# Cross-attention scores of a perceiver layer: sixteen 32x32 fp32 tiles per batch in place of masked three-part matmuls

## The reference, cut to what matters

```
x = x + xattn(layernorm(x), ctx, ctx, mask, Wq, bq, Wk, bk, Wv, bv, Wo, bo)
q = (Q @ Wq.T + bq)  -> 16 heads of 32        # k, v from ctx in the same way
scores = q k^T / sqrt(32) + mask              # [batch, head, 32, 257]
out = softmax(scores) v ;  return out @ Wo.T + bo
```

## Time and profile before

| | us |
|---|---|
| median of 3 runs | 837.57 |
| the runs | 836.25, 837.57, 840.66 |
| the profiled execution, own time | 840.95 |
| its span | 838.9 |
| TensorE busy | 784.2 |
| VectorE busy | 468.3 |
| ScalarE busy | 336.2 |
| GpSimd busy | 301.8 |

### The profile page before, as it was taken

How to read it: one execution, slowest core, us unless ns; L and a number is a source line. 1 busy time by engine, 2 the same in 40 slices (tenths; PEclk the granted TensorE clock), 3 DMA queues, 4 the chain that set the end, 5 groups by cost and what they waited for, 6 DMA issues and landing times. The chain is left out here.

```text
span 838.9 us, 19731 instructions
## 1 busy us (share of the span) xinstructions
PE 784.2 (93%) x7618; PEld 632.4 (75%) x7618; DVE 468.3 (56%) x1000; ACT 336.2 (40%) x686; POOL 301.8 (36%) x375
## 2 busy tenths in 40 slices
PE   2999999999999999999999999769999988999994
PEld 1878888888888888888888887557888766677673
DVE  6725555636555554556465555555676676433556
ACT  2534435443443434344444435322554454622220
POOL 2038023303312330332133130455677671394002
PEclk9999999999999999999999999889999989999998
DMA  8111110110011011101101113130000003100011
GB/s 322 54 47 51 52 52 1 52 50 10 40 50 50 0 50 50 49 1 50 50 3 47 50 50 101 50 90 3 1 0 0 1 8 118 54 0 1 1 50 50
DMA packets 8455, 36.92 MB, mean 44 GB/s; under 512 B 2137, under 2 KB 2393, under 8 KB 5218
## 3 DMA queue, kind: packets, MB, share of 16 engines
q1 hardware_dynamic: 8418, 36.42, 12.1%
HBM read 34.32 MB, written 2.10 MB: 43 GB/s over the span
## 5 line engine op out<-in xcount | busy, mean ns | idle before, releaser
L94 PE MATMUL pj<-W_hi 128*128 128x512 f32 x512 | 206.6, 403 | 0.0
L96 PE MATMUL pj<-W_lo,W_hi 128*128 128x512 f32 x512 | 200.8, 392 | 0.0
L95 PE MATMUL pj<-W_hi,W_lo 128*128 128x512 f32 x512 | 199.7, 390 | 0.0
L640 DVE SCALAR_TENSOR_TENSOR kf_lo<-pj,bk,kf_hi 128x512 fp32r<-128x512 f32 x64 | 48.0, 750 | 120.5 <-ACT kf_hi L477 120.5
L96 PEld LDWEIGHTS pj<-W_lo,W_hi 128*128 128x128 f32 x512 | 96.1, 188 | 21.5
L94 PEld LDWEIGHTS pj<-W_hi 128*128 128x128 f32 x512 | 96.2, 188 | 18.4
L247 POOL CAST kf_hi<-kt_hi 128x8 fp32r (+1 forms) x32 | 6.3, 197 | 287.9 <-PE tp L96 278.4
L95 PEld LDWEIGHTS pj<-W_hi,W_lo 128*128 128x128 f32 x512 | 96.4, 188 | 17.5
L477 ACT ACTIVATE kf_hi<-pj,bk 128x512 fp32r<-128x512 f32 x64 | 44.2, 690 | 134.6 <-PE pj L96 134.6
L484 ACT ACTIVATE V<-pj 128x512 f32<-128x512 f32 x64 | 38.3, 599 | 107.4 <-PE pj L96 107.4
L492 ACT ACTIVATE p_flat<-m_flat,nmax 128x257 f32<-128x257 f32 x128 | 63.8, 501 | 11.6 <-DVE nmax L651 11.6
(11 more groups left out here) (283 smaller groups left out, 1609.7 us busy)
## 6 DMA issues: line engine op xcount, KB each, us to landing
raw<-ctx_dram SPq DMA_DIRECT2D x15, 1024.0 KB, 4.8
raw<-w_dram SPq DMA_DIRECT2D x5, 1024.0 KB, 4.8
raw<-w_dram SPq DMA_DIRECT2D x6, 768.0 KB, 4.3
out_dram<-raw SPq DMA_DIRECT2D x8, 256.0 KB, 2.1
x_nat<-x_dram SPq DMA_DIRECT2D x2, 512.0 KB, 4.7
raw<-wq_dram SPq DMA_DIRECT2D x1, 1024.0 KB, 7.1
x_nat<-x_dram SPq DMA_DIRECT2D x1, 1024.0 KB, 9.1
raw<-wk_dram SPq DMA_DIRECT2D x1, 1024.0 KB, 10.2
```

Of the source, the lines that this page charges most:

```text
L94: eng.matmul(out, a_hi, b_hi, start=first, stop=False)
L95: eng.matmul(out, a_lo, b_hi, start=False, stop=False)
L96: return eng.matmul(out, a_hi, b_lo, start=False, stop=last)
L640: eng.scalar_tensor_tensor(out=K_lo[:, g, :, 0:SM], in0=pj[g % 2][:, :].rearrange("p (j n) -> p j n", j=2), scalar=bk[:, g:g + 1], in1=K_h ...
```

## The change

Each batch's scores become sixteen fp32 matmuls, not split: for row group r (partitions 32r to 32r + 31, the head r of each group) and column group g, weights are 32 channels x 32 queries of `q_b`, the moving operand is 257 columns of K on the same 32 partitions. The result of (r, g) goes to bank `sc[r]`, rows 32g to 32g + 31. So a bank now holds the heads r, 4 + r, 8 + r, 12 + r in place of 4g to 4g + 3. The order is four rounds k, in each r = 0 to 3 with g = (r + k) mod 4; only the four matmuls of the last round raise `s_done`. They wait for all masks of the batch before at once.

What follows from the new order of heads: V's channels are placed by permuted views of Wv as it is split (four pieces in place of one on ScalarE and on VectorE), bv is loaded in four strips, and Wo's rows in four strips of 256 KB. K is kept as one fp32 tensor, evacuated by ScalarE alone; VectorE's `k_evac` and the split of the tail keys go. GpSimd's `q_blocks` becomes one copy per batch, beside one copy of the tail key. `wq_hi` and `wq_lo` get tensors of their own. The mask, softmax, transposes and weighted sum keep their code.

```diff
+        K = sb("K", [P, CT, 2, SK])
+        q_b = [sb(f"q_b{j}", [P, CT, S]) for j in range(2)]
+        def wv_by_tile(c):
+            return wv_raw[:, c, :].rearrange("p (g r d) -> p r g d", g=CT, r=4)
 # SyncE
-            eng.dma_start(bv[:, :], io["bv"]).then_inc(small_in, 16)
+            for g in range(CT):
+                strip, of_strip = bv[g * HD:(g + 1) * HD, :], io["bv"].rearrange("(r d) g -> g d r", d=HD)[g]
+                eng.dma_start(strip, of_strip, allow_slow_non_contiguous=True).then_inc(small_in, 16)
...
+            eng.wait_ge(ctx_lo, NPAIR - 1)
+            for g in range(CT):
+                strip = raw[g * HD:(g + 1) * HD, 0, :].rearrange("p (r n) -> p r n", r=CT)
+                of_strip = io["w5"][0].rearrange("(r d) (g n) -> g d r n", d=HD, g=CT)[g]
+                eng.dma_start(strip, of_strip).then_inc(wo_in, 16)
+            eng.wait_ge(ctx_lo, NPAIR)
+            eng.dma_start(raw[:, 1, :], io["w5"][1]).then_inc(w_in[1], 16)
 # GpSimd, pair(n)
-                need(eng, s_done, 8 * n)
...
+                if isinstance(n, int) and n == 0:
+                    eng.wait_ge(tailT_out, 2)
                 for j in range(2):
-                    for K, kt in ((K_hi, kt_hi), (K_lo, kt_lo)):
-                        eng.tensor_copy(K[:, :, j, SM:KW],
-                                        kt[:, :, bass.ds(2 * n + j, 1)].broadcast_to([P, CT, 2])).then_inc(k_tail, 1)
-                if not first:
-                    q_blocks(n, 0)
-                    q_blocks(n, 1)
+                    b = 2 * n + j
+                    need(eng, s_done, 4 * (b - 1))
+                    eng.tensor_copy(q_b[j][:, :, :], Q_T[:, :, bass.ds(b * S, S)]).then_inc(qb_made, 1)
+                    eng.tensor_copy(K[:, :, j, SM:SK], kt32[:, :, bass.ds(b, 1)]).then_inc(k_tail, 1)
 # TensorE, scores(n, j)
-                for g in range(CT):
-                    need(eng, masked_made, 8 * n + 4 * (j - 1) + g + 1)
-                    if g == 2 and j == 0:
-                        need(eng, pt_act, 2 * n)
-                        need(eng, pt_dve, 2 * n)
-                    three(eng, sc[g][:, 0:KW], Qd_hi[j][:, g, :], Qd_lo[j][:, g, :],
-                          K_hi[:, g, j, :], K_lo[:, g, j, :], True, True).then_inc(s_done, 1)
+                b = 2 * n + j
+                eng.wait_ge(k_out, 4 * n + 4)
+                eng.wait_ge(k_tail, b + 1)
+                eng.wait_ge(qb_made, b + 1)
+                need(eng, masked_made, 4 * b)
+                if j == 0:
+                    need(eng, pt_act, 2 * n)
+                    need(eng, pt_dve, 2 * n)
+                eng.sem_inc(s_ready, 1)
+                for k in range(4):
+                    for r in range(4):
+                        g, rows = (r + k) % CT, slice(r * HD, (r + 1) * HD)
+                        mm = eng.matmul(sc[r][g * S:(g + 1) * S, 0:SK], q_b[j][rows, g, :], K[rows, g, j, :], start=True, stop=True)
+                        if k == 3:
+                            mm.then_inc(s_done, 1)
 # ScalarE
-                eng.activation(K_hi[:, g, :, 0:SM], pj[g % 2][:, :].rearrange("p (j n) -> p j n", j=2),
-                               ACT.Identity, bias=bk[:, g:g + 1]).then_inc(k_hi, 1)
+                eng.activation(K[:, g, :, 0:SM], pj[g % 2][:, :].rearrange("p (j n) -> p j n", j=2),
+                               ACT.Identity, bias=bk[:, g:g + 1]).then_inc(k_out, 1)
...
-            split_hi(wv_hi[:, :, :], wv_raw).then_inc(w_hi, 1)
+            for c in range(CT):
+                split_hi(wv_hi[:, c, :].rearrange("p (r g d) -> p r g d", r=4, g=CT), wv_by_tile(c)).then_inc(wv_made, 1)
+            eng.wait_ge(wv_made, CT)
+            eng.sem_inc(w_hi, 1)
 # VectorE: split_lo of Wv in the same four pieces, and
-            def k_evac(n, g):
-                eng.wait_ge(k_hi, 4 * n + g + 1)
-                eng.scalar_tensor_tensor(out=K_lo[:, g, :, 0:SM], ...
```

More of the change, by code:

```diff
@@ L115, in cross_attention @@
         c_hi, c_lo = [c_hi0, c_hi1], [c_lo0, c_lo1]
[L116 to L121, removed]
+        K = sb("K", [P, CT, 2, SK])
+        wq_hi, wq_lo = (sb(w, [P, CT, D], F32R)[:, :, :] for w in ("wq_hi", "wq_lo"))
         V = sb("V", [P, 4, D])
@@ L130, in cross_attention @@
         tail_nat = P_T[0:B, 0, :, :]
-        Qd_hi = [sb(f"Qd_hi{j}", [P, CT, P], F32R) for j in range(2)]
-        Qd_lo = [sb(f"Qd_lo{j}", [P, CT, P], F32R) for j in range(2)]
         Q_T = sb("Q_T", [P, CT, T])
@@ L165, in cross_attention @@
         bias_made, dve_step = sem("bias_made"), sem("dve_step")
-        ctx_hi, ctx_lo, kv_done, k_hi, k_lo, v_out = (sem(n) for n in ("ctx_hi", "ctx_lo", "kv_done", "k_hi", "k_lo", "v_out"))
-        k_tail, q_hi, q_lo, qd_made = (sem(n) for n in ("k_tail", "q_hi", "q_lo", "qd_made"))
+        ctx_hi, ctx_lo, kv_done, k_out, v_out = (sem(n) for n in ("ctx_hi", "ctx_lo", "kv_done", "k_out", "v_out"))
+        k_tail, qb_made, wv_made, wo_in = sem("k_tail"), sem("qb_made"), sem("wv_made"), sem("wo_in")
+        def wv_by_tile(c):
+            return wv_raw[:, c, :].rearrange("p (g r d) -> p r g d", g=CT, r=4)
         ident_made, heads_made = sem("ident_made"), sem("heads_made")
@@ L260, in _ @@
             pair(0)
-            eng.wait_ge(small_in, 7 * 16)
+            eng.wait_ge(small_in, 10 * 16)
             eng.wait_ge(z_made, NT)
@@ L338, in k_tile @@
                 else:
-                    eng.wait_ge(k_lo, 4 * n + g - 1)
+                    eng.wait_ge(k_out, 4 * n + g - 1)
                 for c in range(CT):
@@ L348, in v_tile @@
                 if t < 2:
-                    eng.wait_ge(k_lo, 4 * n + 3 + t)
+                    eng.wait_ge(k_out, 4 * n + 3 + t)
                 else:
@@ L467, in weight_split @@
             def weight_split(i, used):
-                eng.wait_ge(w_in[i], 16)
+                if i == 0:
+                    eng.wait_ge(wo_in, 4 * 16)
+                else:
+                    eng.wait_ge(w_in[1], 16)
                 eng.wait_ge(kv_done, used)
@@ L512, in pair @@
                 k_evac(n, 2)
-                if first:
-                    tail_keys()
                 k_evac(n, 3)
@@ L686, in pair @@
             def pair(n, p, first, last):
-                k_evac(n, 0)
                 if not first:
                     pt_evac(n - 1, 1)
-                k_evac(n, 1)
-                if not first:
                     o_evac(n - 1, 0)
@@ L712, in _ @@
             eng.wait_ge(w_hi, 3)
-            split_lo(wv_lo[:, :, :], wv_raw, wv_hi[:, :, :]).then_inc(w_lo, 1)
+            for c in range(CT):
+                split_lo(wv_lo[:, c, :].rearrange("p (r g d) -> p r g d", r=4, g=CT), wv_by_tile(c),
+                         wv_hi[:, c, :].rearrange("p (r g d) -> p r g d", r=4, g=CT)).then_inc(wv_made, 1)
+            eng.wait_ge(wv_made, 2 * CT)
+            eng.sem_inc(w_lo, 1)
             eng.wait_ge(w_hi, 4)
-            eng.wait_ge(small_in, 7 * 16)
+            eng.wait_ge(small_in, 10 * 16)
             split_lo(t_lo[:, :, :], tail[:, :, :], t_hi[:, :, :]).then_inc(w_lo, 1)
@@ L1315, in weight_split @@
             def weight_split(i):
-                eng.wait_ge(w_in[i % 2], 16 * (i // 2 + 1))
+                eng.wait_ge(w_in[i % 2], 16 * ((i + 1) // 2))
                 eng.activation(w_hi[i][:, :, :], raw[:, i % 2, :].rearrange("p (c n) -> p c n", c=CT),
```

41 lines of the change are left out of this document (1 added, 40 removed).

## The result

| | before | after |
|---|---|---|
| median of 6 runs, us | 838.14 (835.97 to 840.66) | **824.15** (821.89 to 826.05) |
| ratio | | 0.984 (0.9816 to 0.9864) |
| profiled execution, us (span) | 840.95 (838.9) | 823.83 (822.0) |

A forecast was written before the change was run, and what follows sets the result against it. TensorE was taken to bound the cross-attention loop, busy 406.95 of 407.00 us. Sixteen pairs at 0.98 us gave 15.7, less 0.1 for the last pair: 822 us from a median of 837.57, range 812 to 842.

The forecast's parts named there:

- The block: One batch's scores on TensorE: sixteen fp32 tiles at once take 0.87 us in place of 1.42.
- start spacing: At the score block's beginning: records start 0.0067 us apart or less, so 16 tiles start within 0.10 us.
- change of shape: At the score block's two ends, switching between wide and small matmuls on TensorE: 0.09 + 0.20 us.
- two streams per row group: Rival for the score block: only two records stream per row group, block 1.44 us, total 840 us; chance 0.12.
- row groups in turn: Rival for the score block: a row group's four tiles follow one another, block 2.07 us, total 860 us; chance 0.09.
- halves in program order: Rival for the score block: second halves hold back next tiles, block 4.4 us, total about 935 us; chance 0.04.
- GpSimd's relief: VectorE beside GpSimd without Qd products: four scalings 1.14 us in place of 1.39, dtail 0.29 in place of 1.26.
- The rival without relief: VectorE's scalings stay 1.39 us and dtail may stay: gain 0.61 us a pair, total 828 us; chance 0.06.
- The wait for probabilities: TensorE at a pair's first transposes: a new wait of 0.25 us for VectorE's scalings.
- The pair: Two batches in the cross-attention loop: gain 0.98 us, 0.86 up to the first transposes and 0.12 at L381.
- Costed at nothing: Rest of the change, such as VectorE's K evacuation, Wv's split, bv's and Wo's strips: hidden, charged no time.
- The clock: Later stages: a shift in where the clock falls to 1.2 GHz, allowed 2 us either way.

The follow-up runs named there:

- e9: The changed kernel with VectorE's first-batch scalings before the second batch's masks, plus K and the score queries in bf16, 258 columns: 807.38 us.
- e1: The changed kernel with four GpSimd products a pair put back right behind its copies, into a buffer nobody reads: 907.43 us.
- e2: The kernel before, with GpSimd's Qd products made in the first pair alone, later pairs using the first pair's queries: 836.73 us.
- e3: The changed kernel with VectorE's scalings of a pair's first batch ahead of its second batch's masks, dtail staying behind them: 816.44 us.
- e6: The changed kernel with VectorE's second evacuation of each K tile put back, result unread, and tiles waiting for it: 824.63 us.
- e5: The kernel before, with VectorE's scalings of a pair's first batch ahead of its second batch's masks: 837.0 us.
- e4: The changed kernel without the rotation of tiles, column group g = k in each round: 823.92 us.
- e7: e3 with GpSimd's four products per pair put back right behind its copies, as in e1: 817.62 us.

## Why the prediction was right, point by point

- **The block.** Forecast 0.87 us, measured 0.86. All parts came from rows of other shapes: the columns of fp32 transposes, the start spacing and the change of shape of the earlier trace rows. All sixteen tiles ran at once, so the rivals "two streams per row group", "row groups in turn" and "halves in program order" fall. The first 16 records start within 0.10 us, none in the 0.12 us after that, and 16 more from 0.24 us on. Banks alternate in the timeline by twos (`sc`, `sc`, `tp`, `tp` in program order of r), so the first sixteen are one record of each tile, and a second half comes only after the first half of the last tile; e9, with one record per tile, has no second sixteen. Had each tile's halves held back the next tile, the block would have been 4.4 us by the rival's sum. The Trainium skill ("TensorE: Matmul & The Clock Gate", Part 3, The mechanism) has matmuls start and end strictly in program order. The prediction took that for the halves of fp32 matmuls too, and for these it does not hold here. Of whole matmuls the trace does not contradict it: as far as the banks' names tell, the first halves come in program order, and so do the second halves.
- **GpSimd's relief.** Forecast 1.14 us for four scalings and 0.29 for `dtail`, measured 1.14 and 0.29; `dtail` keeps that in all 32 batches, the scalings in all but two: 2.32 us in the first pair and 2.17 in the 15th. The rival without relief falls. The reason was only half seen: I read longer durations beside a product, not that the engines take turns (e1), and I laid the scalings' 0.25 us to a product though they stay without any product (e2). Products and split are both gone in the changed kernel, so the forecast came out.
- **The wait for probabilities** is the mis-sized term: 0.25 us forecast, measured 357.36 - (356.66 + 0.23) = 0.47, and 0.46 to 0.50 in 13 of the 16 pairs (0.27 in the second; the first and the 15th as told above). Counted from the block's beginning in TensorE's step (353.05 + 0.23 = 353.28): the masks start at 354.38, 1.10 behind it, not 1.03; they take 1.39 to the reciprocal, not 1.44; and from the scalings' end at 357.12 to the transposes go 0.24 us, not 0.05. 0.07 - 0.05 + 0.19 = 0.21 us. The 0.05 was taken from line 381's start behind `dtail` (366.51 to 366.56), where it was the 8 transposes before that covered the rest of the hand-over; the first transposes stand behind an idle TensorE. e3 shows the term's size by removing it.
- **The pair.** Forecast gain 0.98 us, measured 0.80: first scores to first transposes 7.68 (349.68 to 357.36) against 7.49 forecast and 8.35 before; transposes to the next tile's second matmul 1.36 against 1.46 (0.10 of the 0.12 forecast); 0.03 elsewhere.
- **The loop's ends.** Not in the forecast: the 15th pair, 1.03 us longer than its neighbours. The fifteen periods together are 11.1 us shorter (434.71 to 423.59), and the first `pb` comes 0.1 us earlier. The first scores start 0.44 us later (66.63 to 67.07), but that is no more than executions differ in: 65.5 to 67.9 us in the three traces of the old code, 65.8 to 67.7 in those of the new.
- **Costed at nothing:** the K pass (e6), Wv's split in four pieces (2.18 us on ScalarE in place of 1.91, with no wait of TensorE from 24 to 67 us), bv's strips, bo and the Wo strips. In the list of transfers (KB each, us to landing) the strips of Wo are:

```profile
raw<-w_dram SPq DMA_DIRECT2D x4, 256.0 KB, 5.2
```

  Nothing waits for them.
- **The clock.** The later stages made up part of what the loop lacked. I allowed 2 us either way for the clock there; these stages gave 2.7 by the medians. Forecast 15.6, got 14.0: 11.3 in place of 15.6 in the loop, and the later stages the rest. The total came nearer than its main term, by luck. The later stages' code did not change, and their time differs between executions of the same code: from the loop's end on, the same 3170 matmuls take 319.9 us in the profile of the kernel before, 318.5 in e5 and 315.8 in e2, 314.3 in the profile after, and 313.7 to 317.1 in the variants of the new code. How much of the 2.7 us is the change's stays open. e4, whose pair is as after's, came 12.1 us below the kernel before that was measured beside it (823.92 against 835.99).

## What to carry to other kernels

When a block on the busiest engine gets shorter, write down both chains to the next use of its result, from the same start, with the hand-over taken from a row where the waiting engine stood idle; then try the order that lets the late one go first, which here was worth half as much again as the change. Read the first and the last pairs too: other work of GpSimd lay there, and it cost one variant 5.6 us. Before putting work on GpSimd, look which VectorE instructions read SBUF alone beside it: they wait for whole instructions, and its place matters more than its length.

## What the runs showed of the hardware that I had not expected

- Sixteen 32x32 fp32 tiles of 257 columns run all at once: 0.86 us for the block, against 0.46 in bf16 (e9); starts are 0.0067 and 0.0033 us apart.
- An fp32 tile's second half begins 0.24 us behind its first, after the first halves of all other tiles.
- VectorE's scalings (SBUF to SBUF) and GpSimd's products exclude each other by whole instructions (4.19 us in place of 1.14, e1); masks that read PSUM do not (0.42 us beside products, e7). Short GpSimd work seems to count as well: with a `q_b_lo` of 0.55 us beside them and no product, four scalings take 1.39 us (e2).
- The gap of 3.36 us on TensorE was followed by granted clock 0.50 (e1); the gaps of 0.47 us in after, and the 1.30 us of its first pair, left it at 1.00 in the loop.
